# A two-layer transformer tower on one core: expert outputs loaded ahead of the second attention, and its first steps ahead of the last expert's sum

## The reference

```python
# soft mixture: 64 experts, 16 slots each, so 1024 slots for every batch
logits = einsum('bmd,npd->bmnp', x, phi_n)
D = softmax(logits, axis=1)
C = softmax(logits.reshape(b, m, 1024), axis=-1)
Xs = einsum('bmd,bmnp->bnpd', x, D)
...                                          # layer norm, two matrices, gelu: "small experts"
Y = einsum('bsd,bms->bmd', Ys, C)            # every token sums the outputs of all 1024 slots
h = h + Y
h = h + attention(layernorm(h))              # 12 heads of 16, rotary tables
h = h + routed_experts(layernorm(h))         # 8 "large experts", one for each token
```

## Time and profile before

| | |
|---|---|
| median of 3 runs | 1408.03 us (1406.95 to 1409.55) |
| profiled execution | 1409.95 us, span 1408.2 us |
| mean granted clock of PE | 0.986 of full speed |
| PE, ACT, DVE busy in 861 to 868 us | 6.87, 2.07, 0.96 of 7.00 us |
| PE, ACT, DVE busy in 876.6 to 886 us | 8.97, 0.00, 2.66 of 9.40 us |

### The profile page before, as it was taken

One profiled execution on the slowest core, in us unless ns is written; L12 is line 12 of the kernel. 1 busy time (PEld: TensorE's weight loads), 2 busy tenths in 40 slices (PEclk: granted clock), 3 DMA queues, 4 the chain that ended last, 5 costly groups with the idle time before them and its releaser, 6 DMA issues. The chain is left out here.

```text
span 1408.2 us, 29711 instructions
## 1 busy us (share of the span) xinstructions
PE 1332.5 (95%) x9086; PEld 1190.7 (85%) x9086; DVE 971.5 (69%) x2953; ACT 936.1 (66%) x2209; POOL 253.6 (18%) x284
## 2 busy tenths in 40 slices
PE   8799999998999999999999999799999999879995
PEld 6688888886899989998999998688898888768895
DVE  7888877555877777777777773588888888632321
ACT  1488888886666666666666664488888888725551
POOL 5422200001111111111111110012122122111344
PEclk9999999999999999999999999999999999989998
DMA  6144444455666666656665664544454547015631
GB/s 199 45 159 162 162 153 154 157 203 170 196 196 197 186 189 190 200 182 198 190 193 185 193 188 160 160 150 140 154 160 139 152 149 215 15 48 147 158 70 17
DMA packets 181635, 221.04 MB, mean 157 GB/s; under 512 B 25348, under 2 KB 148458, under 8 KB 181536
## 3 DMA queue, kind: packets, MB, share of 16 engines
q1 hardware_dynamic: 147904, 179.52, 41.0%
q10 hardware_dynamic: 25952, 33.32, 7.2%
q0 software_dynamic: 7680, 6.95, 2.7%
HBM read 142.36 MB, written 79.90 MB: 158 GB/s over the span
## 5 line engine op out<-in xcount | busy, mean ns | idle before, releaser
L1246 PE MATMUL bank<-e_w,e_h_full 128*128 128x192 f32 x1920 | 324.7, 326 | 0.4
L1246 PEld LDWEIGHTS bank<-e_w,e_h_full 128*128 128x128 f32 x1920 | 310.6, 190 | 1.7 <-ACT e_h_full L1319 1.3
L1319 ACT ACTIVATE e_h_full<-bank,e_b 128x512 f32<-128x512 f32 x240 | 165.2, 689 | 191.5 <-PE bank L60 191.5
L1180 POOL TENSOR_TENSOR e_ln_rstd<-e_ln_var_eps,minus_half 128x4 f32<-128x4 f32 x62 | 62.5, 1008 | 450.6 <-DVE e_ln_var_eps L1369 450.6
L1727 ACT ACTIVATE probs<-bank,head_neg_max 128x128 f32<-128x128 f32 x384 | 134.9, 393 | 7.6 <-DVE head_neg_max L1823 5.7
L1376 DVE TENSOR_SCALAR e_rows<-e_slot_sums,e_ln_mean_var,e_ln_rstd 128x192 f32<-128x192 f32 x248 | 77.5, 376 | 77.6 <-POOL e_ln_rstd L1180 77.6
L1289 ACT ACTIVATE e_x_full<-bank,e_ln_shift,e_ln_gain 128x512 f32<-128x512 f32 x124 | 89.7, 774 | 44.8 <-PE bank L1218 44.8
L1002 PE MATMUL bank<-x,dispatch_weights 128*128 128x193 f32 x512 | 95.7, 329 | 6.9 <-ACT slot_stage L845 5.9
L60 PE MATMUL bank<-e_x_hi,e_w1hi 128*128 128x512 f32 x216 | 95.4, 442 | 2.3 <-ACT e_h_full L1319 1.2
L1607 PE MATMUL bank<-slot_outputs_then_w_part,combineT 128*128 128x193 f32 x512 | 94.0, 336 | 2.5 <-ACT combineT L1719 2.1
L1404 DVE TENSOR_TENSOR e_stage<-bank,e_b 128x768 f32<-128x768 f32 x64 | 61.3, 957 | 46.5 <-PE bank L1246 46.4
(11 more groups left out here) (285 smaller groups left out, 3081.7 us busy)
## 6 DMA issues: line engine op xcount, KB each, us to landing
slot_sums<-slot_stage SPq DMA_DIRECT2D x64, 386.0 KB, 3.2
e_slot_sums<-slot_sums SPq DMA_DIRECT2D x64, 386.0 KB, 3.6
slot_outputs<-e_stage ACTq DMA_DIRECT2D x64, 384.0 KB, 3.2
slot_outputs_then_w_part<-slot_outputs SPq DMA_DIRECT2D x32, 768.0 KB, 4.8
e_w<-in_w SPq DMA_DIRECT2D x64, 288.0 KB, 2.9
slot_logits<-kept_logits SPq DMA_DIRECT2D x32, 512.0 KB, 3.0
slot_logits<-slot_logits SPq DMA_DIRECT2D x32, 512.0 KB, 3.4
e_w1raw<-in_w SPq DMA_DIRECT2D x80, 192.0 KB, 2.7
```

The lines of the kernel that those rows point to most:

```text
L1180: pool.tensor_tensor(rs[u][:], ve[u][:], half[:], ALU.pow).then_inc(rstd_ready, 1)
L1246: last = pe.matmul(ybank(u)[:, j // 2, (j % 2) * D:(j % 2 + 1) * D], hf[:, k, js], w2s[u][:, k, :], start=k == 0, stop=k == MT - 1)
L1319: act.activation(hf[:, m, :], hbank(u, m), act_fn, bias=b1s[:, m, ds(n, 1)]).then_inc(acted, 1)
```

## The change

Seven edits, all around the passage from the small experts to attention:

- The tiles for the expert outputs belong to `CombineLoads` now, so they exist during the small experts; POOL fills their columns of ones there.
- SP loads chunks 0 to 6 (experts 0 to 55) of batches 0 and 1 at the end of the small experts, behind the logits and ahead of the rotary tables, once the stores of these experts are counted. The eighth chunk follows at the beginning of attention's block, once all stores are counted. PE waits for it right before the last chunk of `Y`.
- ACT runs `then.scalar` (weights, exponential of batch 0) ahead of the store of the last expert, and no longer waits for the stores at the block's end.
- DVE runs `then.vector` (maxima, weights) ahead of the last expert's sum.
- PE's fillers at the passage go from 20 to 8 and from 18 to 2.
- DVE's constants that need the router's weights go to the start of turn 3, two small fills of `v_by_head` to the start of turn 1.
- The semaphore `ones_set` is split; the part for `v_by_head` is called `values_padded`.

```diff
+        self.slots = [sb(f"slot_outputs_then_w1_part{k}", [P, NC * (D + 1)]) for k in range(2)]
+        self.ysb = [w[:].rearrange("p (c d) -> p c d", c=NC) for w in self.slots]
...
+    def load_outputs(self, sp, b, chunks, done):
+        ys = self.T["ys"][:, b, :].rearrange("(c p) d -> p c d", p=P)
+        sp.dma_start(self.ysb[b % 2][:, chunks, 0:D], ys[:, chunks, :]).then_inc(done[b % 2], 16)
+
+    def first_outputs(self, sp, stored):
+        for u in range(2):
+            sp.wait_ge(stored[u], 16 * (NE0 - NE0 // NC) // 2)
+        for b in range(2):
+            self.load_outputs(sp, b, slice(0, NC - 1), self.ys_in)
+
+    def last_outputs(self, sp):
+        for u in range(2):
+            sp.wait_ge(self.stored[u], 16 * NE0 // 2)
+        for b in range(2):
+            self.load_outputs(sp, b, slice(NC - 1, NC), self.ys_last_in)
...
         for b in range(2):
             self.load_logits(sp, b)
+        self.first_outputs(sp, stored)
         sp.dma_start(self.cos[:], ins["cos"]).then_inc(self.tables_in, 16)
...
+    def gpsimd(self, pool):
+        for u in range(2):
+            pool.memset(self.ysb[u][:, :, D:], 1.0).then_inc(self.ones_set, 1)
...
                 if not routed:
-                    keep_busy(pe, T, hbank(0, 0), 20)
+                    keep_busy(pe, T, hbank(0, 0), 8)
...
                 each_pair(act, turn)
-                send(n_exp - 1, 1)
                 if then is not None:
                     then.scalar(act)
-                if not routed:
-                    for u in range(2):
-                        act.wait_ge(stored[u], 16 * turns)
+                send(n_exp - 1, 1)
...
+                        if then is not None and isinstance(n, int) and n == n_exp - 1:
+                            then.vector(dve)
                         dve.wait_ge(b2_in[u], 16 * (i + 1))
...
-                if then is not None:
-                    then.vector(dve)
...
-                load_outputs(0)
+                    early.load_outputs(sp, b, slice(0, NC), ys_in)
+
+                early.last_outputs(sp)
 
                 def turn(t, u, n, y, q, a, p, r, z, w):
-                    if t + 1 < NB:
+                    if 2 <= t + 1 < NB:
                         load_outputs(t + 1)
...
                         if y == 0:
-                            keep_busy(pe, T, bank[:, 6, :], 18)
-                            pe.wait_ge(S["ones_set"], 4)
+                            keep_busy(pe, T, bank[:, 6, :], 2)
+                            pe.wait_ge(S["ones_set"], 2)
...
                         for c in range(NC):
+                            if y < 2 and c == NC - 1:
+                                pe.wait_ge(early.ys_last_in[u], 16)
                             last = pe.matmul(bank[:, 0, 0:D + 1], cT[:, c, :], ysb[u][:, c, :],
...
+                    if t == 1:
+                        dve.wait_ge(S["values_padded"], 2)
+                        for k in range(2):
+                            dve.memset(vs[k][:, 8, HD:HD + 1], 1.0).then_inc(S["values_padded"], 1)
+                    if t == 3:
+                        dve.wait_ge(router_in, 64)
+                        dve.tensor_scalar(limit[:], rank[:], float(NE1 + 1), -float(CAP), ALU.subtract, ALU.mult)
...
-                dve.wait_ge(S["ones_set"], 4)
-                for u in range(2):
-                    dve.memset(vs[u][:, 8, HD:HD + 1], 1.0)
                 st.did(dve.memset(so_far_wide[:], 0.0))
-                dve.wait_ge(router_in, 64)
-                dve.tensor_scalar(limit[:], rank[:], float(NE1 + 1), -float(CAP), ALU.subtract, ALU.mult)
```

More of the change, by code:

```diff
@@ L167, in tower_program @@
                     large = ExpertLoads(Alloc(nc, c4), al, "e1", NE1, H1, T["xm"], ins["w1_1"], ins["b1_1"],
-                                        ins["w2_1"])
+                                        ins["w2_1"], slots=early.slots)
                     large.xf, large.xhi, large.xlo, large.xst = small.xf, small.xhi, small.xlo, small.xst
@@ L175, with __init__ @@
 class ExpertLoads:
-    def __init__(self, sb_of, sem_of, name, n_exp, hid, rows, w1, b1T, w2, ln=None):
+    def __init__(self, sb_of, sem_of, name, n_exp, hid, rows, w1, b1T, w2, ln=None, slots=None):
         sb = lambda n, *a: sb_of.sb(f"{name}_{n}", *a)
@@ L206, in __init__ @@
         else:
-            self.slots = [sb(f"slot_outputs_then_w1_part{k}", [P, NC * (D + 1)]) for k in range(2)]
-            parts = [w[:, 0:2 * hid].bitcast(F32R).rearrange("p (k h) -> p k h", k=2) for w in self.slots]
+            parts = [w[:, 0:2 * hid].bitcast(F32R).rearrange("p (k h) -> p k h", k=2) for w in slots]
             self.w1hi = [sb("w1hi0", [P, 2, hid], F32R), parts[0]]
@@ L323, in __init__ @@
         self.Wp = sb("Wproj_two_parts", [P, 2, D])
+        self.slots = [sb(f"slot_outputs_then_w1_part{k}", [P, NC * (D + 1)]) for k in range(2)]
+        self.ysb = [w[:].rearrange("p (c d) -> p c d", c=NC) for w in self.slots]
+        self.ys_in, self.ones_set = [sem(f"slot_out_in{u}") for u in range(2)], sem("ones_set")
+        self.ys_last_in = [sem(f"last_slots_out_in{u}") for u in range(2)]
     def load_logits(self, sp, b):
@@ L327, in load_logits, with sync @@
         sp.dma_start(self.nmb[b % 2][:], self.T["nm_rows"][b, :].partition_broadcast(P)).then_inc(self.lg_in[b % 2], 16)
-    def sync(self, sp):
+    def load_outputs(self, sp, b, chunks, done):
[11 more added lines that the diff above has]
+            self.load_outputs(sp, b, slice(NC - 1, NC), self.ys_last_in)
+    def sync(self, sp, stored):
         ins = self.ins
+        self.stored = stored
         for k, rows in ((0, slice(0, P)), (1, slice(0, DR)), (1, slice(DR, P))):
@@ L1167, in _ @@
                 if then is not None:
-                    then.sync(sp)
+                    then.sync(sp, stored)
             if ln is not None:
@@ L1184, in _ @@
                     turn(turns - 1)
+                    then.gpsimd(pool)
             if routed:
@@ L1435, in combine_phase @@
         cos, sin, rank, numbers = early.cos, early.sin, early.rank, early.numbers
-        ysb = [w[:].rearrange("p (c d) -> p c d", c=NC) for w in large.slots]
+        ysb = early.ysb
         cinv = sb("row_inv", [P, 1])
@@ L1469, in combine_phase @@
         tables_in, router_in, lg_in = early.tables_in, early.router_in, early.lg_in
-        ys_in = [sem(f"slot_out_in{u}") for u in range(2)]
+        ys_in = early.ys_in
         out_stored, steps = sem("out_stored"), sem("combine_vector_steps")
@@ L1473, in combine_phase @@
         S = {n: sem(n) for n in (
-            "ones_set", "padded", "pool_tables", "router_cleared", "Y_done",
+            "values_padded", "padded", "pool_tables", "router_cleared", "Y_done",
             "h2_ready", "ln4_var", "ln4_rstd", "ln5_var", "ln5_rstd", "x4_ready", "x4T_done", "x4_hi_ready", "x4_split",
@@ L1479, in combine_phase @@
             "router_exped", "chosen", "counted", "counts_read", "placed", "numbered")}
-        S.update(W_split=early.W_split, C_ready=early.C_ready, C_exp=early.C_exp)
+        S.update(ones_set=early.ones_set, W_split=early.W_split, C_ready=early.C_ready, C_exp=early.C_exp)
         head_out, head_inv = bank[:, 1, 0:2 * P], bank[:, 2, 0:2 * P]
@@ L1762, in turn @@
                         if q == 0:
-                            act.wait_ge(S["ones_set"], 4)
+                            act.wait_ge(S["values_padded"], 4)
                         act.wait_ge(S["v_done"], q + 1)
@@ L1818, in turn @@
                 def turn(t, u, n, y, q, a, p, r, z, w):
+                    if t == 1:
[5 more added lines that the diff above has]
+                        dve.tensor_scalar(limit[:], rank[:], float(NE1 + 1), -float(CAP), ALU.subtract, ALU.mult)
+                        st.wait()
+                        st.did(dve.tensor_scalar(so_far[0:1, 0, :], rank[0:1, :], float(NE1), -float(CAP),
+                                                 ALU.subtract, ALU.mult))
+                        st.wait()
                     if a is not None:
@@ L1950, in _ @@
                 dve.memset(onehot_wide[:], 0.0)
-                dve.wait_ge(S["ones_set"], 4)
-                for u in range(2):
-                    dve.memset(vs[u][:, 8, HD:HD + 1], 1.0)
                 st.did(dve.memset(so_far_wide[:], 0.0))
-                dve.wait_ge(router_in, 64)
-                dve.tensor_scalar(limit[:], rank[:], float(NE1 + 1), -float(CAP), ALU.subtract, ALU.mult)
-                st.wait()
-                st.did(dve.tensor_scalar(so_far[0:1, 0, :], rank[0:1, :], float(NE1), -float(CAP), ALU.subtract,
-                                         ALU.mult))
-                st.wait()
                 each_turn(turn)
```

5 lines of the change are left out of this document (1 added, 4 removed).

## The result

| | before | after |
|---|---|---|
| median of 12 runs each, in turn on one chip | 1410.37 us (1406.95 to 1412.78) | 1404.65 us (1402.09 to 1414.42) |
| ratio, 95% interval | | 0.9963 (0.9948 to 0.9978) |
| profiled execution | 1409.95 us, span 1408.2 | 1403.08 us, span 1401.3 |

The changed kernel is faster, but 1404.65 us lies above the forecast of 1399.3 us and 0.65 us outside the range. The two intervals overlap.

The account below looks back on a forecast made before the run. Bound: late expert outputs (Y(0) ending 884.26) and DVE (885.31, after waiting for the router) at the passage to attention. Terms -8.5 + 0.35 - 0.6 = -8.75 us, from 1408.03 to 1399.3 us; range 1396.8 to 1404.0.

Parts of the forecast that it names:

- The term of -8.5: Passage to attention: DVE takes up Y(0) at about 876.8 instead of 885.31, and everything behind moves along: -8.5 us.
- the last piece: SP's 96 KB load of the eighth output chunk behind expert 63's store: 2.4 us to land, at 876.25.
- the cover of `Wqkv_lo`: DVE before the last expert's sum: `Wqkv_lo` ends 1.15 us before `e_stage` begins, so the moves cost nothing.
- the queue: SP's loads at the small experts' end: early output loads add 4.3 us, draining at about 872 instead of 868.
- Rival A: Last piece is late, 6.3 us to land, so Y(0) gains only 4.55 us: 1403.8 us, chance 0.12.
- The base: Starting time of the sum: 1408.03 us, the median of the runs shown; the profiled execution took 1409.95.
- Turn 3 and turn 1: DVE's moved constants and waits: +0.35 us ahead of turn 3's `head_neg_max`; two tiny fills in turn 1 cost 0.
- The clock term: PE in Y(1): a shorter first pause may keep 2.4 GHz (-1.55 us) or not (0); taken as -0.6 us.
- B: Fewer fillers around the barrier drop PE to 1.2 GHz, slowing Y(0) and turn 1's fillers: 1404.0 us, chance 0.09.
- C: Nothing is won: a last piece of 10.4 us ends Y(0) at 884.85: 1408.0 us, chance 0.05.
- D: Slower: a late `Wqkv_lo` delays the last `e_stage`, store and barrier; at 882.2 it makes 1410.9 us, chance 0.04.

Follow-up runs that it names:

- e8: Changed kernel with all eight output chunks of both batches loaded behind the last store, none early: 1411.02 us, ratio to before 1.0003.
- e11: Changed kernel with weights, maxima and first exponential behind the last sum and last store again: 1408.01 us, ratio to before 0.9983.
- e10: Kernel before with only the two router constants and their wait moved to turn 3: 1408.28 us, ratio to before 0.9987.
- e4: Changed kernel with DVE's router wait and two constants back at the start of turn 0: 1406.71 us, one run.
- e15: Changed kernel with odd experts' weights at their old address, five fillers ahead of Y(1), seven ahead of turn 1's transposes: 1400.75 us, ratio to before 0.9935.
- e7: Changed kernel with the two first-weight tiles of the odd experts at their old address: 1402.12 us, ratio to before 0.9939.
- e9: Kernel before with only the two tiles of outputs allocated early, as the change does: 1412.04 us, ratio to before 1.0011.
- e14: Changed kernel with odd experts' weights at their old address, measured in the fourth batch: 1401.89 us, ratio to before 0.9948.
- e13: Changed kernel, unchanged, measured again in the fourth batch on another chip: 1402.92 us, ratio to before 0.9951.
- e1: Kernel before with one unused tile of 64 bytes a partition behind the tiles of CombineLoads: 1413.64 us, ratio to before 1.0019.
- e5: Kernel before once more, unchanged: 1411.34 us, one run.
- e6: Changed kernel once more, unchanged: 1403.19 us, one run.
- e2: Changed kernel with the same unused 64 bytes a partition: 1403.66 us, ratio to before 0.9950.

## Why the prediction was right and wrong

**Right: the passage.** On the axis of before (1.17 us taken off), attention begins at 873.43 (forecast 873.3), Y(0) ends at 876.8 (876.8), and DVE takes it up at 876.84 (876.8). The term of -8.5 measured -8.39. Below it, the store landed in 2.6 us (2.3), the last piece in 2.0 (2.4), and the cover of `Wqkv_lo` was 1.26 us (1.15). Y(1) began at 881.63 (881.5). The formula in the Trainium skill ("DMA: Bandwidth & Descriptors", section on the anatomy of one DMA), given for loads that GpSimd issues, had made the last piece an estimated 2.2 us; the trace, where SP issues it, agrees within 0.2. e8, e11 and e10 show that the parts don't add up: without the early loads 7.4 us at `row_inv` are lost, without the early exponential 5.9, and the router's part alone gave 0.83.

**Wrong, but harmless: the queue.** "The queue drains at about 872": the window 868 to 872 moved 345 GB/s, and the last two small loads of SP's list, issued at 867.72 and 868.25, took 6.6 and 6.5 us, until 874.8 (873.6 on the axis of before). Y(0) was not held up.

**Rival A in small.** A last piece that is late, by 0.34 and 0.82 us, was seen in two profiles (e4, e15), never by the 4 us that A supposed, and in e15 by the store and not by the load. The piece took 2.0 to 2.2 us in both.

**The step that failed: a term is missing from the sum, and its base is too low.** The moved tiles were named in the change and priced at nothing, since no instruction moved. They shift the odd experts' weights, and every odd expert then takes 0.04 us longer: +1.17 us in the profile, shown both ways by e7 and e9. In the total times it is +1.0 in the medians of e14 and e13 and +1.7 in those of before and e9, neither clear of noise by itself. The order of the instructions doesn't show it, and neither does any wait of PE; only the addresses of before and of the change, side by side, differ there. The base, below, makes up more of the miss, 2.3 us. With both put right the sum gives 1402.7 us, and its range, moved as far, holds the 1404.65.

**Turn 3 and turn 1.** The constants in turn 3 cost nothing, where +0.35 was forecast: from `row_inv` of batch 2 to that of batch 3 it is 9.94 us after and 9.95 before. In turn 1, priced at 0, all profiles with the constants in turn 3 (e10 too, where nothing else is changed) show 0.3 us more, at DVE's `ln_mean_var`:

```profile
889.55 0.18 DVE L1920 BATCH_NORM_AGGREGATE ln_mean_var<-ln_stats 128x2 f32<-128x6 f32 x1 [0.21 <-DVE rope_crossed L1917]
```

In before and in e1, e4, e5 and e9, whose constants stand ahead of the first turn or in it, this idle time is not there. Why the place of the constants decides it stays open. The two errors cancel.

**The clock term.** -0.6 us stood for a chance. The profiled execution had none of it (4.44 us), and the argument that the first pause is shorter now was right (0.61 instead of 1.54 us). In the four profiles with the instructions of before (before, e1, e5, e9; first pause 1.29 to 1.79 us) Y(1) fell to the lower clock each time, 4.26 to 5.49 us; of the six with the changed ones (0.61 to 0.65 us) three ran it at 2.4 GHz. But e10, with a first pause of 0.62 us, fell too (4.50 us), and in e6 and e13 turn 1 fell instead or as well. From batch 0 to batch 2, before, e5 and e9 take 20.64, 20.54 and 20.51 us and e1 23.44; with the 0.3 of turn 1 that they don't have this is some 20.9 without e1 and 21.6 with it. The six average 20.71. So the clock gave 0.2 us on average if e1 is left out and 0.9 if it is counted. So few profiles neither confirm the 0.6 nor refute it.

**The base.** I took the sum from 1408.03 us, the median of three runs, although the profiled execution took 1409.95. Five batches with 11 to 29 runs put before at 1409.44 to 1410.53. So 2.3 of the 5.35 us by which the time was missed are the base, and 3.0 are a smaller gain (5.7 for 8.75). Of these the placement is 1.0 to 1.2, the clock between -0.3 and +0.4, and turns 1 and 3 together 0 (+0.3 and -0.35 against the forecast). The other 1.4 to 2.3 us aren't traced to a cause, but they are within the first measurement's interval: the second measurement of the same kernel gives 6.5 (medians) or 6.9 us (ratio), and the measured terms, -8.4 + 1.2 + 0.3 and -0.2 to -0.9 for the clock, come to -7.1 to -7.8. The second measurement's 1402.92 us would have lain inside the range, so on which side of its upper end the result fell was also chance. Which executions of the first measurement were dearer, and where, isn't known, since they left no trace; one of them, 1414.42 us, had a mean granted clock of 0.944 instead of 0.983 to 0.987.

**The other rivals.** B didn't come about at the barrier, where PE stood 1.16 us; e8 and e11 show its price behind 4.57 and 4.40 us. C, nothing won, is what e8 measured, by another way than a last piece of 10.4 us: with the early loads gone. D's cover held. Two slips in the sums change nothing: by A's times for DVE, C would gain 0.46 us and not 0.35, and the range begins at 1396.9 and not 1396.8.

## What to carry to other kernels

When a stall has two causes that end within a microsecond of each other, remove both in one go, and test each alone to know what it was worth: here the router's part gave 0.8 us by itself, and all of the change without the early loads gave nothing in the total. A change that only allocates a tile earlier can move others and change the speed of a loop far away from it; compare addresses, not only instructions. Take the base of a forecast from the profiled execution as well as from a median of few runs.

## What was not expected of the hardware

- Of the 15 matmuls of an odd expert's first product, all but the first followed each other by 0.2326 to 0.2335 us on average in the ten profiles in which the tiles that hold the weights lay at byte 142016, 142080 or 129728 of the partitions, and by 0.2304 to 0.2313 in before, e5 and e10, where they lay at 129664; 64 bytes were enough. In the fast cases both tiles, as those of the even experts, begin 128 bytes past a multiple of 256, in the slow ones 0 or 192 bytes past one. That is an observation on four addresses, in e1, e2 and e9 with other tiles moved as well (e7 sets the weights apart from them); the rule behind it stays open.
- Behind an idle time of 4.4 to 4.6 us PE ran Y(0) at 1.2 GHz (5.48 and 5.01 us for 16 rows), behind 1.16 us never (2.79 to 3.08 us in the profiles with that pause in which Y(0) had nothing to wait for). Behind the small pauses of turn 0 (0.61 and 1.47 us) it went either way in executions of one and the same kernel; behind 1.29 to 1.79 and 1.46 us it fell in all four profiles.
